# First loads, regrouped heads, a new order, and the rows of maxima issued by ScalarE

## The chip, the core and the metric

One core of one Trainium2 chip. The metric is the device time of one execution in microseconds (us), lower is better. The kernel before takes 883.62 us (median of three runs, 883.47 to 884.68).

## What is computed

Two transformer layers over x of shape (4, 512, 256), batch j being one of four sequences, 16 heads of 16 channels, MLP width 1024. Both layers modulate their norms by a condition vector per batch:

```python
# layer 0
g1, g2, s1, s2, sh1, sh2 = split(silu(cond) @ ada_w.T + ada_b, 6)
h = layernorm(x) * (1 + s1) + sh1
q, k, v = split(h @ qkv_w.T + qkv_b); q, k = rope(q), rope(k)
x = x + (softmax(q k^T / 4) v @ proj_w.T + proj_b) * g1
h2 = layernorm(x) * (1 + s2) + sh2
x = x + (gelu(h2 @ fc1_w.T + fc1_b) @ fc2_w.T + fc2_b) * g2
# layer 1: shift1, scale1, shift2, scale2 = split(swiglu(cond @ w_t1 + b_t1) @ w_t2 + b_t2, 4)
x = x + mha(rmsnorm(x, g1) * (1 + scale1) + shift1)      # rope on even/odd channels
x = x + swiglu(rmsnorm(x, g2) * (1 + scale2) + shift2 ...) @ w_fo + b_fo
```

## The kernel before

**Units and quads.** The work is 8 units (a batch in a layer: units 0 to 3 are layer 0, 4 to 7 layer 1), and each unit's attention is 4 quads of 4 heads, 32 quads in all. A unit has a part before attention (`pre_pieces`: norm, the products qk and v, rope), the quads, and a part after (`post_pieces`: output projection, residual, norm, MLP). The steady schedule runs a unit's quads beside the post part of the unit before and the pre part of the unit after.

**A quad.** TensorE makes 16 products `peaks` (L805), of which VectorE takes a row maximum each into `top` (L1066). `top_turn` (L780) transposes these, ScalarE copies the result into `top_t` (L1280), and two small transfers write it as one more row of the stacked q in `qt`, one for each half of the partitions (`top_row`, L716). 16 products `scores` (L792) then give q k^T with the maximum subtracted, ScalarE takes the exponential (L1290) into `pr`, which has room for 8, and TensorE accumulates `values` (L819) in `ps_o`. `output` copies, transposes (L830) and divides.

**Rope and the round trip.** Heads are grouped for rope in two pairs of chunks. Per pair: ScalarE takes the two chunks (`take`, L1261), VectorE and GpSimd multiply by cosine and sine (L1044, L1381), VectorE adds (L1053), ScalarE makes the high part (`high`, L1271), GpSimd the low part (L1392), and SP spills them to DRAM in four transfers (`spill`, L691 and L694). `fill(n)` reads quad n from there into `qt` and `kt`, which have room for three quads (L708). In the kernel before each quad takes two heads of either pair, so the fill of a unit's first quad waits for both pairs.

**Buffers.** Six PSUM banks (`ring`) are handed to the products in the order of the program; each engine waits for the one it needs by counts.

**Order.** `program()` (L438) is one list of pieces, each with its engine. Every engine runs its own pieces strictly in the order of that list, so a wait on one piece holds all later pieces of the same engine. The list is `first_pieces`, `first_steps`, and then all pieces with hand-given ticks (`QUAD_AT`, `PRE_AT`, `POST_AT`, `SPLIT_AT`), sorted; a quad advances by SQ = 28 ticks.

**The start.** A first block (`prologue`, L1459 to L1515) issues 16 loads on SP, fills constants, and computes silu(cond) and its broadcasts `wide`. It ends for all engines together. Then the main block begins with `mod_0` (L953, 32 matmuls of the modulation), the norm of unit 0, `gates` (L916, one per batch), qk, v, `net_1` and `net_2` (L927, L941: layer 1's condition network).

Of the kernel before, what the change touches and what calls it, by code (L numbers as in the profile page):

```python
# [12 lines left out]
P = 128  # L13
# [85 lines left out]
SQ = 28  # L99
# [8 lines left out]
def first_pieces():  # L108

    def gates(b):  # L110
        return [("pe", "gates", b), ("dve", "gates", b)]

    pieces = [("dve", "norm_stats", 0, 0), ("dve", "norm_var", 0, 0), ("pool", "root", 0, 0),
              ("dve", "norm_rows", 0, 0), ("pe", "mod_0"), ("dve", "mod_0")]
    pieces += gates(0) + [("pe", "norm_turn", 0, 0)] + gates(1)
    pieces += [("act", "modulated", 0, 0, k) for k in range(KC)]
    for pair in range(2):
        for c in (2 * pair, 2 * pair + 1):
            pieces += [("pe", "qk", 0, c), ("act", "take", 0, c)]
        pieces += rope_pieces(0, pair)  # L120
    pieces += [("sp", "fill", 0), ("sp", "fill", 1)]
    for t in range(T):
        pieces += [("pe", "v", 0, t), ("dve", "take_v", 0, t)]
    pieces += gates(2) + [("pe", "net_1")]
    return pieces


def first_steps():

    beside = {0: [("dve", "net_1"), ("act", "net_gate"), ("pe", "gates", 3)],  # L130
              1: [("dve", "net_gate")], 3: [("dve", "gates", 3)],
              3 + NET_PARTS: [("dve", "net_2")]}
    steps = [("sp", "load_x", 2)]
    for i in range(T * QUAD):
        steps.append((None, "peaks", 0, i))
        steps += beside.get(i, [])
        if 2 < i < 3 + NET_PARTS:
            steps.append(("pe", "net_2", i - 3))
    return steps + [("sp", "load_x", 3)] + top_pieces(0)


def top_pieces(n):

    return [("pe", "top", n), ("act", "top", n), ("sp", "top", n)]


def quad_pieces(n):
# [20 lines left out]
PRE_AT = ({'norm': (-80, -50, -19, -33, -12, -8, -2),  # L168
  'qk': (-5, 4, 11, 30),
  'v': (14, 23, 29, 64),  # L170
  'take': (1, 4, 26, 29),
  'take_v': (15, 26, 26, 59),
  'rope': ((8, -4, 11, 12, -2, 9), (38, 40, 39, 45, 50, 37))},
 {'norm': (-10, -1, -17, 4, 9, 12, 12),
  'qk': (14, 14, 25, 28),
  'v': (14, 15, 16, 19),
  'take': (12, 12, 27, 31),
  'take_v': (14, 17, 18, 21),
  'rope': ((18, 9, 19, 25, 13, 22), (28, 18, 34, 44, 48, 66))},
 {'norm': (-12, -3, -1, 7, 10, 10, 10),  # L180
  'qk': (17, 17, 22, 22),
  'v': (22, 23, 24, 24),
  'take': (16, 17, 21, 23),
  'take_v': (22, 23, 24, 24),
  'rope': ((17, 27, 18, 21, 30, 39), (35, 27, 36, 41, 50, 52))})
# [3 lines left out]
POST_AT = ({'o': (-1, -1, -1),  # L189
  'project': (1, 6, 8, 8),  # L190
  'proj': (9, 4, 9, 4),
  'norm': (14, 16, 11, 21, 32, 32, 32),
  'split': (38, 38, 37, 43),
  'up': (41, 41, 45, 45, 50, 50, 56, 60, 67, 68, 75, 76, 85, 86, 92, 93),
  'after_up': (0, 2, 2, 5, 2),
  'down': (47, 50, 53, 56, 61, 64, 71, 74, 82, 82, 84, 92, 97, 98, 106, 111),
  'after_down': (1, 5)},
 {'o': (-1, -1, -1),
  'project': (3, 10, 10, 10),
  'proj': (9, 10, 10, 15),  # L200
  'norm': (16, 16, 26, 19, 29, 25, 27),
  'split': (30, 35, 39, 43),
# [1379 lines left out]
```

## Time and profile before

| | us |
|---|---|
| median of 3 runs | 883.62 |
| profiled execution | 884.96 |
| its span, first to last instruction | 883.2 |

```profile
## 1 busy us (share of the span) xinstructions
PE 804.7 (91%) x4800; PEld 493.7 (56%) x4800; DVE 636.5 (72%) x1348; ACT 491.3 (56%) x1015; POOL 290.4 (33%) x263
## 2 busy tenths in 40 slices
PE   2908999899999999999999999999999999999497
DVE  3225864679897889887988788888868788864344
ACT  0200555556874687558665777766547655666132
PEclk9955786799999999999999999999999999999799
## 4 chain that ended last, share of the span: by engine, by line
PE 71%; DVE 11%; issue 6%; POOL 4%; DMA 3%; ACT 2%; SPq 1%; POOLq 0%; DVEq 0%; ACTq 0%
```

PE is TensorE, PEld its weight loads, DVE VectorE, ACT ScalarE, POOL GpSimd, SPq the SP queue that issues transfers. In part 2 each digit is the busy share of a slice of 22 us in tenths, and PEclk the clock that TensorE was granted in tenths of full speed (10 shows as 9). The first two and a half slices and the slices 3 to 9 are where the rows differ from the rest. Part 4 shares out the chain of work that ended last.

### The profile page before, as it was taken

To read this page: it belongs to the slowest core of one execution; us is meant where nothing else is said; L and a number is where in the kernel's file an instruction comes from. 1 tells how busy PE (TensorE), PEld (TensorE's weight loads), DVE (VectorE), ACT (ScalarE), POOL (GpSimd) and SP (SyncE) were. 2 spreads that over 40 slices of the span, in tenths; PEclk is the share of its full clock that TensorE was granted. 3 is DMA by queue.
4 is the path that set the end of the run, shared out by engine and by line. 5 is a ranking of instruction groups with operands and counts; after the bars stand their busy time and mean duration, and the time that the engine had idled before them with its cause. 6 is when DMAs were issued, how large, how long until landed. Compare 5 with 4: busy or idle time off the path is not lost.

```text
span 883.2 us, 14213 instructions
## 1 busy us (share of the span) xinstructions
PE 804.7 (91%) x4800; PEld 493.7 (56%) x4800; DVE 636.5 (72%) x1348; ACT 491.3 (56%) x1015; POOL 290.4 (33%) x263
## 2 busy tenths in 40 slices
PE   2908999899999999999999999999999999999497
PEld 2504333254665466556654666466856775677396
DVE  3225864679897889887988788888868788864344
ACT  0200555556874687558665777766547655666132
POOL 0310131034345433443345333631244222222234
PEclk9955786799999999999999999999999999999799
DMA  8372244414411441144114413453104502100000
GB/s 318 118 215 55 70 134 130 99 48 132 134 37 37 132 132 37 40 129 132 38 37 131 133 38 85 128 148 73 37 26 132 148 21 60 37 2 1 24 2 25
DMA packets 33480, 76.26 MB, mean 86 GB/s; under 512 B 4480, under 2 KB 9216, under 8 KB 33024
## 3 DMA queue, kind: packets, MB, share of 16 engines
q1 hardware_dynamic: 33408, 75.35, 30.4%
q8 instruction: 39, 0.64, 0.3%
q14 instruction: 33, 0.27, 0.1%
HBM read 39.42 MB, written 35.65 MB: 85 GB/s over the span
## 4 chain that ended last, share of the span: by engine, by line
PE 71%; DVE 11%; issue 6%; POOL 4%; DMA 3%; ACT 2%; SPq 1%; POOLq 0%; DVEq 0%; ACTq 0%
PE ring L888 16%; PE ps_o L819 12%; PE ps_b L905 11%; PE ring L805 8%; PE ring L792 8%; DVE top L1066 6%; PE ring L757 4%; PE ring L858 3%; POOL sines L1381 2%; PE ring L770 2%; PE ring L830 1%; DMA scratch<-low 1%; DMA kt<-scratch 1%; PE ring L739 1%; PE ring L916 1%
## 5 line engine op out<-in xcount | busy, mean ns | idle before, releaser
L1066 DVE TENSOR_REDUCE top<-ring 128x1 f32<-128x512 f32 x512 | 322.4, 682 | 71.1 <-PE ring L805 69.7
L1290 ACT ACTIVATE pr<-ring 128x512 f32<-128x512 f32 x512 | 268.5, 608 | 71.7 <-PE ring L792 62.0
L1422 POOL TENSOR_TENSOR act_l<-mlp,act_h 128x256 fp32r<-128x256 f32 x128 | 100.7, 787 | 270.3 <-DVE act_h L1143 270.3
L805 PE MATMUL ring<-kt,qt 48*128 48x512 f32 x512 | 136.9, 482 | 26.4 <-DMA kt<-scratch 23.4
L819 PE MATMUL ps_o<-pr,va 128*17 128x512 f32 x1024 | 143.1, 645 | 0.2
L792 PE MATMUL ring<-qt,kt 49*128 49x512 f32 x512 | 126.4, 470 | 6.8 <-DMA qt<-top_t 2.5
L805 PEld LDWEIGHTS ring<-kt,qt 48*128 48x128 f32 x512 | 59.4, 195 | 105.5 <-issue 68.0
L1324 ACT ACTIVATE mlp<-ring,col 128x256 f32<-128x256 f32 x128 | 61.2, 478 | 99.7 <-PE ring L888 73.5
L792 PEld LDWEIGHTS ring<-qt,kt 49*128 49x128 f32 x512 | 55.3, 192 | 74.9 <-issue 48.3
L888 PE MATMUL ring<-hh,wl 128*128 128x256 f32 x384 | 83.5, 299 | 5.9 <-issue 3.5
L905 PE MATMUL ps_b<-wh,act_l 128*128 128x256 f32 x256 | 79.8, 312 | 1.2 <-POOL act_l L1422 0.8
L1129 DVE SCALAR_TENSOR_TENSOR mlp<-mlp 128x256 f32<-128x256 f32 x128 | 56.7, 443 | 33.3 <-ACT mlp L1329 30.2
L888 PE MATMUL ring<-hh,wh 128*128 128x256 f32 x384 | 78.3, 286 | 0.0
L888 PE MATMUL ring<-hl,wh 128*128 128x256 f32 x384 | 78.3, 286 | 0.0
L905 PE MATMUL ps_b<-wl,act_h 128*128 128x256 f32 x256 | 72.2, 282 | 0.0
L905 PE MATMUL ps_b<-wh,act_h 128*128 128x256 f32 x256 | 72.0, 281 | 0.0
L888 PEld LDWEIGHTS ring<-hh,wl 128*128 128x128 f32 x384 | 60.0, 193 | 21.0 <-issue 16.4
L1381 POOL TENSOR_TENSOR sines<-raw,trig 128x1024 f32<-128x1024 f32 x16 | 44.9, 2807 | 61.1 <-ACT raw L1261 30.1
L905 PEld LDWEIGHTS ps_b<-wh,act_l 128*128 128x128 f32 x256 | 48.5, 189 | 26.9 <-issue 24.1
L888 PEld LDWEIGHTS ring<-hh,wh 128*128 128x128 f32 x384 | 60.9, 195 | 0.0
L888 PEld LDWEIGHTS ring<-hl,wh 128*128 128x128 f32 x384 | 60.6, 194 | 0.0
L757 PE MATMUL ring<-hf,wf 128*128 128x512 f32 x128 | 59.5, 604 | 0.0
(91 smaller groups left out, 1038.2 us busy)
## 6 DMA issues: line engine op xcount, KB each, us to landing
scratch<-high SPq DMA_DIRECT2D x48, 512.0 KB, 5.0
qt<-scratch SPq DMA_DIRECT2D x64, 192.0 KB, 3.5
kt<-scratch SPq DMA_DIRECT2D x64, 192.0 KB, 4.4
scratch<-low SPq DMA_DIRECT2D x16, 512.0 KB, 5.9
mlp<-in_w_split SPq DMA_DIRECT2D x20, 256.0 KB, 3.2
xs<-in_x SPq DMA_DIRECT2D x4, 512.0 KB, 8.4
wf<-in_w_f SPq DMA_DIRECT2D x2, 1024.0 KB, 11.7
out_x<-xs SPq DMA_DIRECT2D x4, 512.0 KB, 2.9
```

The lines of the kernel that those rows point to most:

```text
L757: last = nc.tensor.matmul(bank[:, :], w[:, k, c * P:(c + 1) * P], hf[:, k, :], start=(k == 0), stop=(k == KC - 1))
L792: nc.tensor.matmul(bank[:, :], kt[r:r + SHIFT + 1, n % NSLOT, h // 2, t * P:(t + 1) * P], qt[r:r + SHIFT + 1, n % NSLOT, h // 2, :], start ...
L805: nc.tensor.matmul(bank[:, :], qt[r:r + SHIFT, n % NSLOT, h // 2, t * P:(t + 1) * P], kt[r:r + SHIFT, n % NSLOT, h // 2, :], start=True, s ...
L819: last = nc.tensor.matmul(ps_o[32 * h:32 * h + HD + 1, :], va[:, u % 2, t, QUAD * g + h, :], pr[:, slot, :], start=(t == 0), stop=(t == T ...
L888: last = nc.tensor.matmul(bank[:, s * TH:(s + 1) * TH], wp[:, k, c:c + P], hp[:, k, half * TH:(half + 1) * TH], start=(n == 0), stop=(n == ...
L905: last = nc.tensor.matmul(ps_b[:, s * C:(s + 1) * C], ap[:, at % 2, s * P:(s + 1) * P], wp[:, f, :], start=(f == 0 and s == 0 and n == 0), ...
L1066: nc.vector.tensor_reduce(top[:, n % 2, c:c + 1], bank[:, :], AX_X, ALU.max, negate=True).then_inc(free, 1)
L1129: step(nc.vector.scalar_tensor_tensor(val[at % 2], aux[at % 2], 1.0, val[at % 2], ALU.add, ALU.mult))
L1290: nc.scalar.activation(pr[:, at % NP, :], bank[:, :], ACT.Exp, scale=SCALE).then_inc(free, 1)
L1324: nc.scalar.activation(val[at % 2], src, ACT.Identity, bias=col[:, c:c + 1]).then_inc(val_in, 1)
L1381: nc.gpsimd.tensor_tensor(sines[:, :, :], raw[:, :, :], trig[:, 1, :].unsqueeze(1).to_broadcast([P, 2, L]), ALU.mult).then_inc(sin_in, 1)
L1422: nc.gpsimd.tensor_tensor(act_l[:, at % 2, :], src, act_h[:, at % 2, :].bitcast(F32), ALU.subtract).then_inc(act_l_in, 1)
```

## The change

**First loads.** The prologue's block issues 6 loads only, in a new order: cond, x of batch 0, the first third of the modulation weights (now stored so that norm 1's scale and shift come first), cols, identity, and the qkv weights of layer 0. The other loads are pieces of SP's program (`load`). `mod_0` is split in two halves of 16 matmuls. silu, `half_gate` and the broadcasts `wide` (`widen`) become pieces. The weights of the condition network and of the gates move to other buffers, with a semaphore each.

**Regrouping.** The heads of the qkv weights are reordered so that pair 0 holds the heads of quads 0 and 1 and pair 1 those of quads 2 and 3. Fill n waits for the spill of its own pair only.

**Order.** All tick tables are new, with 112 ticks to a quad. The first pieces and all loads have ticks of their own (`FIRST_AT`, `LOAD_AT`) and are sorted in with the rest. TensorE's list now begins mod_0(0), norm_turn(0), qk 0, qk 1, v 0, v 1, qk 2, net_1, v 2, mod_0(1), qk 3, net_2(0), net_2(1), v 3, gates 0 to 3, net_2(2), net_2(3), peaks of quad 0 (with the rest of net_2 between them). SP's begins trig, ada1, ada2, wf0, t1, w_split 0, row, grow, t2, spill(0,0), x1, fill(0), w_split 1, fill(1), spill(0,1). TensorE's last stretch, from the last exponentials on, keeps its sequence but for a few `up` and `down` steps that trade places.

**Rows of maxima.** The piece ("sp", "top") is gone. ScalarE, after its copy into `top_t`, waits for that copy and issues both transfers itself.

The diff, cut to its core (the tick tables left out):

```diff
-SQ = 28
+SQ = 112
...
-    return [("pe", "top", n), ("act", "top", n), ("sp", "top", n)]
+    return [("pe", "top", n), ("act", "top", n)]
...
-    out = []
+    out = [(tick, *piece) for tick, piece in zip(FIRST_AT, first_pieces())]
+    out += [(tick, "sp", "load", name) for name, tick in LOAD_AT.items()]
...
-    return first_pieces() + first_steps() + [p[1:] for p in sorted(ticked(), key=lambda p: p[0])]
+    return [p[1:] for p in sorted(ticked(), key=lambda p: p[0])]
...
+                def load(name):
+
+                    if name in ("x1", "x2", "x3"):
+                        j = int(name[1])
+                        if j == 2:
+                            sp.wait_ge(*filled("net_1"))
+                        if j == 3:
+                            sp.wait_ge(*filled("gates", B - 1))
+                        sp.dma_start(xs[:, j], x_v[j]).then_inc(x_in[j], 16)
+                    elif name == "wf1":
+
+                        sp.wait_ge(*filled("net_2"))
+                        sp.dma_start(wf[:, NWF // 2:NWF], w_f32[:, NWF // 2:NWF]).then_inc(s_wf[2], 16)
...
                     u, g = quad_of(n)
-                    if g == 0:
-                        for pair in range(2):
-                            sp.wait_ge(*spill_landed(u, pair))
+                    sp.wait_ge(*spill_landed(u, g // 2))
...
-                                         scratch[u % 2, :, 8 * op + 2 * g + e, op:op + 3].rearrange(
+                                         scratch[u % 2, g // 2, 2 * op + g % 2, :, e, op:op + 3].rearrange(
                                              "a s d f t -> (s d f) a t")).then_inc(slot_in[n % NSLOT], 16)
-
-                def top_row(n):
-
-                    sp.wait_ge(*emptied("top", n))
-                    for e in range(2):
-                        sp.dma_start(qt[STACK * e + SHIFT:STACK * e + SHIFT + 1, n % NSLOT, :, :].bitcast(F32),
-                                     top_t[8 * e:8 * e + 8, n % 2, :].bitcast(F32)).then_inc(top_in[n % 2], 16)
...
-                def mod_0():
+                def mod_0(m):
...
-                    pe.wait_ge(s_ada, 16)
-                    for n in range(4 * KC):
+                    pe.wait_ge(s_ada[m], 16)
+                    for n in range(2 * KC):
...
                     nc.scalar.activation(top_t[:, n % 2, :], bank[0:T * QUAD, 0:P], ACT.Copy).then_inc(free, 1)
+                    ac.wait_ge(free, before + 1)
+                    for e in range(2):
+                        nc.scalar.dma_start(qt[STACK * e + SHIFT:STACK * e + SHIFT + 1, n % NSLOT, :, :].bitcast(F32),
+                                            top_t[8 * e:8 * e + 8, n % 2, :].bitcast(F32)).then_inc(top_in[n % 2], 16)
...
+            sp.dma_start(cond, cond_t.rearrange("p (k b) -> p k b", k=KC)).then_inc(s_small[0], 16)
             sp.dma_start(xs[:, 0], x_v[0]).then_inc(x_in[0], 16)
+            sp.dma_start(ada[:, :, 0:2 * C], ada_v[:, :, 0:2 * C]).then_inc(s_ada[0], 16)
+            sp.dma_start(col[:, :], cols).then_inc(s_small[1], 16)
+            sp.dma_start(eye[:, :], ident).then_inc(s_small[2], 16)
+            sp.dma_start(wf[:, 0:PROJ[0]], w_f32[:, 0:PROJ[0]]).then_inc(s_wf[0], 16)
...
-                for g in range(NQ):
-                    for e in range(2):
-                        h = g * QUAD + pair * 2 + e
-                        order.append(op * C + h * HD + halves[layer][half * HALF:(half + 1) * HALF])
+                for h in range(2 * QUAD * pair, 2 * QUAD * (pair + 1)):
+                    order.append(op * C + h * HD + halves[layer][half * HALF:(half + 1) * HALF])
```

## Rows read from the trace of the kernel before

**Rows 1.** Busy time by stage: window, its length, each engine, PEclk, DMA, GB/s

```profile
0.00:16.16 16.16, 0.00 (x1) 0.03 (x1) 4.96 (x15) 1.49 (x2) 0.55 (x7) 1.00 0.81 290
16.16:44.20 28.04, 27.62 (x100) 18.85 (x100) 9.38 (x23) 5.03 (x7) 8.87 (x5) 1.00 0.48 177
44.20:64.75 20.55, 0.01 (x2) 0.03 (x1) 4.74 (x8) 1.06 (x1) 2.78 (x2) 0.51 0.73 215
64.75:90.03 25.28, 19.60 (x57) 11.76 (x58) 14.19 (x32) 0.48 (x2) 0.00 (x0) 0.57 0.25 62
90.03:183.31 93.28, 84.99 (x334) 33.88 (x335) 62.10 (x115) 50.17 (x96) 12.24 (x6) 0.75 0.40 107
183.31:272.00 88.69, 87.59 (x544) 51.68 (x544) 76.05 (x165) 62.53 (x134) 37.64 (x34) 1.00 0.33 88
820.00:883.20 63.20, 45.09 (x320) 42.63 (x320) 27.48 (x69) 16.09 (x36) 22.05 (x24) 0.87 0.05 18
```

**Rows 2.** The same view over two longer stretches

```profile
64.75:183.31 118.56, 104.59 (x391) 45.64 (x392) 76.30 (x146) 50.65 (x98) 12.24 (x6) 0.71 0.37 98
183.31:820.00 636.69, 627.40 (x3990) 386.54 (x3989) 513.62 (x1092) 416.98 (x872) 243.86 (x220) 0.99 0.29 78
```

**Rows 3.** Timeline of the first block: start, length, engine, line, operation

```profile
0.72 0.40 SPq L1465 DMA_DIRECT2D o<-in_cond_t  x1
1.19 0.41 SPq L1465 DMA_DIRECT2D col<-in_cols  x1
...
4.64 0.27 DVE L1504 MEMSET top<- 128x256 f32 x1
...
15.28 0.43 SPq L1476 DMA_DIRECT2D wf<-in_w_f  x1
```

**Rows 4.** Waits of TensorE for transfers: total us, times, longest; whole span, then 183 to 820

```profile
PE ring L805 <- DMA kt<-scratch: 23.4, 2, 20.5
...
PE ring L792 <- DMA qt<-top_t: 0.6, 1, 0.6
```

**Rows 5.** The chain of waits from 16 to 66 us: start, length, what

```profile
16.16 6.96 PE ring L953 x32
...
29.80 3.45 PE ring L757 x8
...
42.78 5.89 DMA scratch<-low
...
52.58 5.99 DMA scratch<-low
...
59.98 4.63 DMA kt<-scratch
```

**Rows 6.** Busy time, as rows 1, of two short stretches of the first loads

```profile
4.00:8.00 4.00, 0.00 (x0) 0.00 (x0) 1.01 (x4) 0.10 (x1) 0.00 (x0) 1.00 1.00 290
8.00:12.00 4.00, 0.00 (x0) 0.00 (x0) 1.49 (x11) 0.11 (x1) 0.00 (x0) 1.00 0.99 397
```

**Rows 7.** Timeline of the setup of unit 0, 17 to 72 us

```profile
17.59 0.38 DVE L994 BATCH_NORM_AGGREGATE mv<-stats 128x2 f32<-128x6 f32 x4
19.45 1.38 DVE L1015 TENSOR_SCALAR xn<-xs,mv,rstd 128x256 f32<-128x256 f32 x4 [1.48 <-POOL rstd L1370]
22.98 3.76 PE L916 MATMUL ring<-pr,o 128*128 128x512 f32 x4
23.16 0.19 DVE L1205 TENSOR_TENSOR o<-ring,col 128x32 f32<-128x32 f32 x1 [2.32 <-PE ring L953]
26.53 1.54 PE L739 MATMUL ring<-eye,xn 128*128 128x128 f32 x8
27.70 1.45 ACT L1247 ACTIVATE hf<-ring,mod 128x512 f32<-128x512 f32 x2 [19.59 <-PE ring L739]
27.91 1.88 PE L916 MATMUL ring<-pr,o 128*128 128x512 f32 x4
31.55 0.69 ACT L1261 ACTIVATE raw<-ring,col 128x512 f32<-128x512 f32 x1 [2.41 <-PE ring L757]
36.50 3.62 PE L770 MATMUL ring<-wf,hf 128*128 128x256 f32 x16
42.36 1.84 PE L927 MATMUL ring<-o,xs 128*128 128x4 f32 x16
71.48 0.68 DVE L1164 TENSOR_TENSOR gate<-ring,add 128x512 f32<-128x512 f32 x1
```

**Rows 8.** The issues of the rows of maxima: ns min/median/max, first and last start

```profile
L716 SPq DMA_DIRECT2D qt<-top_t x64: 623/646/774, 87.3 to 801.4; - x64
L1280 ACT ACTIVATE top_t<-ring x32: 249/251/268, 87.0 to 800.5; 16x128 fp32r<-16x128 f32 x32
```

**Rows 9.** SP's longest wait (total, times, longest), and one landing in the chain

```profile
SPq L716 <- ACT top_t L1280: 390.2, 31, 31.1
...
287.80 2.52 DMA qt<-top_t
```

More of the change, by code:

```diff
@@ L108, in first_pieces @@
 def first_pieces():
[L110 to L115, printed above, removed]
+    pieces = [("act", "silu"), ("dve", "half_gate"), ("dve", "silu"), ("pe", "mod_0", 0), ("dve", "norm_stats", 0, 0),
+              ("dve", "norm_var", 0, 0), ("pool", "root", 0, 0), ("dve", "mod_0", 0), ("dve", "norm_rows", 0, 0),
+              ("pe", "norm_turn", 0, 0)]
     pieces += [("act", "modulated", 0, 0, k) for k in range(KC)]
@@ L119, in first_pieces @@
             pieces += [("pe", "qk", 0, c), ("act", "take", 0, c)]
[L120 to L139, printed above, removed]
+        pieces += rope_pieces(0, pair) + [("sp", "fill", pair)]
+        if pair == 0:
+            for t in range(T):
+                pieces += [("pe", "v", 0, t), ("dve", "take_v", 0, t)]
+    pieces += [("pe", "mod_0", 1), ("dve", "mod_0", 1)]
+    for b in range(B):
+        pieces += [("dve", "widen", b), ("pe", "gates", b), ("dve", "gates", b)]
+    pieces += [("pe", "net_1"), ("dve", "net_1"), ("act", "net_gate"), ("dve", "net_gate")]
+    return pieces + [("pe", "net_2", part) for part in range(NET_PARTS)] + [("dve", "net_2")]
+FIRST_AT = (-1462,
+ -798,
+ -1447,
+ -1309,
+ -1227,
+ -1155,
+ -1302,
+ -1156,
+ -1101,
+ -1172,
+ -1416,
+ -1230,
+ -1145,
+ -829,
+ -1042,
+ -808,
+ -1053,
+ -1090,
+ -865,
+ -801,
+ -780,
+ -746,
+ -656,
+ -910,
+ -835,
+ -892,
+ -816,
+ -815,
+ -666,
+ -608,
+ -601,
+ -887,
+ -669,
+ -725,
+ -488,
+ -644,
+ -611,
+ -595,
+ -487,
+ -604,
+ -601,
+ -608,
+ -763,
+ -668,
+ -833,
+ -543,
+ -600,
+ -670,
+ -525,
+ -527,
+ -600,
+ -523,
+ -464,
+ -589,
+ -471,
+ -413,
+ -816,
+ -696,
+ -702,
+ -652,
+ -668,
+ -626,
+ -417,
+ -411,
+ -337,
+ -322,
+ -261,
+ -165,
+ -156)
 def top_pieces(n):
-    return [("pe", "top", n), ("act", "top", n), ("sp", "top", n)]
+    return [("pe", "top", n), ("act", "top", n)]
 def quad_pieces(n):
@@ L414, in pieces_beside @@
     if u == 0:
[L415 removed]
+        out += split_pieces(range(NPLACE), SPLIT_AT[0])
     if u == B + 1:
[L418 to L419 removed]
+        out += split_pieces(range(NPLACE, NCHUNK), SPLIT_AT[1])
     if u >= 1:
@@ L1452, in name @@
     def name(n):
         return sem("pre_" + n)
-    s_small, s_ada, s_t, s_row = (name(n) for n in ("small", "ada", "t", "row"))
-    s_wf = [name("wf0"), name("wf1")]
-    fill, silu_in, dve = (name(n) for n in ("fill", "silu_in", "dve"))
+    s_small = [name("cond"), name("col"), name("eye")]
+    s_ada = [name(f"ada{i}") for i in range(3)]
+    s_wf = [name(f"wf{i}") for i in range(3)]
+    fill = name("fill")
     with nc.Block() as block:
```

597 lines of the change are left out of this document (316 added, 281 removed).

## The prediction

> **What bounds the kernel now.** I read the span by stages first [rows 1]. The table cuts it where the work changes, and the reader is to see four regimes. From 0 to 16.16 us TensorE does nothing. From 16.16 to 44.20 it is busy with the first unit's setup. From 44.20 to 64.75 it is idle again, and its granted clock stands at the lower of its two levels. From 64.75 to 183.31 (attention of unit 0) it is nominally busy 104.6 of 118.6 us, but at a mean clock of 0.71 [rows 2]. From 183.31 to 820 it is busy 627.4 of 636.7 us at 0.99: there TensorE is the bound and only 9.3 us are idle. The last 63.2 us are a chain for the last unit. So whatever does not cut TensorE's own work can win only in the first 183 us, and can lose anywhere.
>
> Next I read what ends the idle stretches. At 16.16 TensorE and VectorE both start, although nothing they need arrives then: the SP queue has just issued its sixteenth load (15.28 plus 0.43 us), and the first program block ends for all engines together [rows 3]. At 64.75 the releaser is a transfer into kt; 20.5 us of TensorE's 23.4 us of waiting on such transfers lie here [rows 4]. The chain behind it [rows 5] runs: hf of unit 0 written by 29.15, pair 0 rotated and spilled (landed 48.67), then pair 1 (landed 58.57), and only then the fills, because the old fill of a unit's first quad waits for both pairs.
>
> **Part 1, the first loads.** After the change the first block issues 6 loads, not 16. At the 0.47 us spacing of these issues [rows 3] they end near 3.5 us; VectorE's three memsets end at 4.91 [rows 3], so the block ends near 5.2. x of batch 0 and the first third of the modulation weights are the second and third load, 1.0 MB together. At the 397 GB/s of the 8 to 12 us stretch [rows 6] that is 2.6 us, and with the slower start of the 4 to 8 us stretch I put the second of them at 7.0. The product mod_0 then has 16 matmuls, not 32: half of 6.96 us [rows 5], done at 10.5. VectorE's three small operations on it take about 0.5 us (estimate: the first of them starts 0.2 after the product and takes 0.19 [rows 7]). Its order puts the variance behind them, so 11.0. From there norm_var to the end of norm_rows took 3.24 us (17.59 to 20.83), and turn to the end of hf 2.62 us (26.53 to 29.15) [rows 7]: 16.9, against 29.15. Gain 12.2 us; the gate product that stood ahead of the turn is moved behind. One thing is paid back. The same four gate matmuls took 3.76 us at 22.98 and 1.88 at 27.91 [rows 7], so TensorE ran at half speed for its first 10 us or so, whatever the clock column says there. Now it starts with less work and gaps, and qk 0 and 1 (3.45 us at full speed, twice that at half) will be met in part: I add 2.0 us, between nothing and 3.45. The nine loads issued by SP from its program, 4.6 MB or 12 us at that rate, end near 20 us, before the first spill; the price if they did not is in the rivals.
>
> **Part 2, regrouping.** Quads 0 and 1 now need only rope pair 0. The first fill no longer waits from 48.67 to 58.57 [rows 5]: 9.9 us. The sizes of spills and fills stay. Sum of parts 1 and 2: first peaks at 64.75 - 12.2 + 2.0 - 9.9 = 44.7. What is late next is TensorE itself. After qk 0 and 1 (near 22.4) it has v (3.62 us), qk 2 and 3 (3.45 [rows 5]), net_1 (1.84 for 16 small matmuls), the second mod_0 (16 of the same kind, 1.84), four gates (4 x 1.88) and half of net_2 (16 more, 1.84): 20.1 us [rows 7], so until 42.5. It fits, and the idle 20.55 us of before are filled. For units 1 to 7 the same relaxation is worth nothing: in 183 to 820 the rows show no wait of TensorE for a fill.
>
> **Part 3, the attention of unit 0.** The stage of 118.56 us holds 76.3 us of VectorE work [rows 2]; a gate (0.68 us [rows 7]) and net_1's small ones leave it, some 1.3 us: 75.0. In the steady stage VectorE is busy 76.05 of 88.69 us, 86% [rows 1]: by that share the stage takes 87.5 us. TensorE's work there is 19.6 x 0.57 + 85.0 x 0.75 = 75 us of full clock, less 3.7 for a gate and half of net_2 that left: 71. At the old mean of the main part, 0.75, it takes 95 us. The lower clock followed the long idle stretch, which is gone, but with VectorE pacing the peaks TensorE will still stand idle in pieces, and the rows show the clock at 0.75 for 93 us after the idle stretch had long ended. So I take 92, between the two and nearer the second. Gain 26.6 us. Ends: 84 us if VectorE reaches 90%, and 114 us if it stays at the 67% (62.10 of 93.28) of before.
>
> The Trainium skill, "TensorE: Matmul & The Clock Gate", section "HAM oscillation — how this bites in real kernels", says that a kernel whose matmuls come in bursts between waits keeps falling back to the lower clock; the low rows of 64.75 to 183.31 agree. By that rule alone the stage would stay as long as before; that is the first rival below.
>
> **Part 4, the rows of maxima on ScalarE.** 64 transfers leave SP. Each issue took 646 ns (623 to 774) on SP [rows 8]. SP waited 390 us for these copies [rows 9], with fills, spills and weight loads queued behind; those now pass. But TensorE waited for a row only 0.6 us in 183 to 820 [rows 4], so nothing is returned. The new cost lies on ScalarE: per quad two issues (1.29 us) and a wait for its own copy (0.26 us): 1.55 us, 50 us over 32 quads. No row shows an issue on ScalarE, so this is bounded by SP's. Behind the wait are the next exps, and TensorE waits for their banks. ScalarE is busy 62.53 of 88.69 us and would come to 68.7, still 20 us short of TensorE, and by the new ticks the copy stands some 55 of a quad's 112 ticks, 11 us, ahead of the scores that need its row. Ends for the 28 steady quads: nothing, or the whole 1.55 each, 43 us. It is nearest to the first, since TensorE's idle time there is 9.3 us in all though ScalarE works through its list in 0.6 us steps and more all the while [rows 7]: I take 0.2 per quad, 6 us.
>
> The landing itself took 2.52 us after the issue [rows 9]. The Trainium skill, "DMA: Bandwidth & Descriptors", section "Issuing engines are not separate DMA queues", speaks against this part: another issuing engine saves only issue time. By it this part is worth 0 or less, as taken.
>
> **Part 5, the new order.** All ticks are new and four times as fine; all 1.5% of idle time in the steady stage is what it can return, and a bad order can cost as much. Between -9 and +9 I take -3. The tail's order on TensorE hardly differs (a few up and down steps trade places), so its 63.2 us stay: 0.
>
> **The sum**: 883.2 - 12.2 + 2.0 - 9.9 - 26.6 + 6 - 3 = 839.5 us of span. The profiled execution took 884.96, the median of the runs is 883.62, 0.4 above the span. Forecast: 840 us.
>
> **The rivals.**
> First, the clock stays low: VectorE keeps 67%, the stage takes 114 us: gain 4.6 instead of 26.6, so 862. For it: the clock rows. Against: part of the low clock followed one idle stretch that goes.
> Second, ScalarE's blocks reach TensorE in part: 0.8 us per steady quad, 22 us instead of 6: 856. For it: ScalarE sits between TensorE's scores and TensorE's values in both directions.
> Third, slower than before: each of the 32 rows stalls TensorE for its whole block and one more hand-over, together over 1.6 us. Without part 4 the sum is 833.5; 32 x 1.6 = 51 gives 885, so from 1.6 us per row it decides, and at 1.75 it is 890. Against: 20 us of free ScalarE time in each unit.
> Fourth, better: the stage takes 84 us, ScalarE costs nothing, and the order returns 6: 883.2 - 20.1 - 34.6 - 6 = 822.5, so 823.
> Fifth, the change doesn't do what it says at the start: the loads put on SP stand in front of the first spill, or TensorE's filling work runs over, and the 9.9 us are lost: 850.
>
> **How the numbers follow.** Forecast (832 to 849) 0.50; first rival 0.15; second 0.12; third 0.04; fourth 0.13; fifth 0.06. The range leaves out the third and the outer part of the fourth and first: 822 to 861. A difference of 0.2%, 1.8 us, is about what a measurement can tell here; all cases but the third are faster: 0.95 faster, 0.01 same, 0.04 slower.
>
> **What would show it.** VectorE's first norm_stats near 6 us, hf of unit 0 near 17, the first peaks near 45, with TensorE busy until then: parts 1 and 2. The first projection of unit 0 (183.31 before) near 137: part 3; if near 159, the clock, to be seen as a mean near 0.75 and VectorE at 67%. From there to the end of the attention near 637 us again; if it is 650 or more and TensorE waits on exps just behind the copies of the row of maxima, part 4 was sized wrong. Issues on ScalarE's queue far from 0.65 us would move that term. It would all be wrong if the new order makes an engine wait in line for something late, which no row of before can show.

## The result, and the profile after

The changed kernel takes 843.38 us (median of 4 runs, 839.93 to 845.36), against 884.15 for the kernel before in the same job (883.47 to 885.35): ratio 0.9533, 95% interval 0.9497 to 0.957. The forecast was 840 with a range of 822 to 861. The profiled execution took 844.6 us with a span of 842.7. In the experiments below the medians and ranges as measured are of all runs and the ratios of the fast ones; four_issues and one_issue have one slow run each (884.43 and 829.1), without which their medians are 873.5 and 821.58, and every price worked out for them goes by these two.

I cut the span at the same points of the work as before: first `peaks`, first `project`, last turn of an output. The lines of the stages of after (core 0; stretch, its length, busy time and instructions of TensorE, its weight loads, VectorE, ScalarE and GpSimd, then granted clock, share of the DMA queues, GB/s):

```profile
0.00:7.03 7.03, 0.00 (x0) 0.00 (x0) 3.77 (x6) 1.49 (x2) 0.55 (x7) 1.00 0.67 207
7.03:46.15 39.12, 32.24 (x121) 21.09 (x121) 15.68 (x53) 7.03 (x10) 14.08 (x8) 0.96 0.70 233
46.15:135.21 89.06, 81.15 (x370) 35.92 (x370) 71.17 (x131) 49.77 (x95) 8.33 (x6) 0.81 0.54 158
135.21:780.24 645.03, 621.73 (x3991) 387.86 (x3991) 517.93 (x1091) 417.31 (x873) 245.23 (x220) 0.98 0.28 78
780.24:842.66 62.42, 43.98 (x322) 41.84 (x320) 28.00 (x70) 16.07 (x36) 22.27 (x24) 0.88 0.05 18
```

and the steady stretch of the kernel before, cut at the same turn (which is 0.7 us before the end of the longer one in [rows 2]):

```profile
183.31:819.30 635.99, 627.12 (x3989) 386.50 (x3989) 513.27 (x1090) 416.98 (x872) 243.86 (x220) 0.99 0.29 78
```

| stage | before | forecast | after |
|---|---|---|---|
| to the first peaks | 64.75 | 44.7 | 46.15 |
| attention of unit 0 | 118.6 | 92 | 89.1 |
| steady stretch | 636.0 | 639 | 645.0 |
| last part | 63.9 | 63.9 | 62.4 |

So 48 us came out of the first two stages and 9 went back in the steady one. There TensorE stands idle for 23.3 us, where it was 8.9 before. What it waits for in that stretch (engine and line that wait, what they wait for: us in total, times, longest):

```profile
PE ring L886 <- DMA qt<-top_t: 4.0, 2, 3.3
PE ps_o L913 <- ACT pr L1425: 3.2, 5, 1.0
PE ring L899 <- ACT mlp L1466: 2.5, 3, 0.8
PE ps_b L999 <- POOL act_l L1569: 2.2, 4, 1.0
PE ring L982 <- POOL hl L1562: 2.0, 4, 0.8
PE ring L886 <- DVE mlp L1242: 1.5, 2, 0.8
```

L886 is now `scores`, L899 `peaks`, L913 `values`, L982 and L999 the two MLP products. ScalarE (ACT) is behind the second and third row, and it feeds the engines in the fourth and sixth. It now also issues the rows of maxima of the first row. One quad in the timeline of ScalarE (start, duration, engine, line, operation, and in brackets idle time before it):

```profile
290.17 0.42 ACT L1475 ACTIVATE mlp<-mlp 128x256 f32<-128x256 f32 x1 [0.67 <-DVE mlp L1255]
290.58 0.27 ACT L1411 ACTIVATE top_t<-ring 16x128 fp32r<-16x128 f32 x1
290.88 1.32 ACTq L1414 DMA_DIRECT2D qt<-top_t  x2
292.32 0.47 ACT L1462 ACTIVATE mlp<-ring,col 128x256 f32<-128x256 f32 x1 [1.47 <-DVE act_h L1248]
```

From the end of the copy to ScalarE's next instruction pass 1.47 us, nearly all of them issuing. This is no harmless place: the chain of work that ended last runs through both issues here and on into the MLP's activation (start, us, what):

```profile
290.58 0.27 ACT top_t L1411
...
290.88 0.66 ACTq L1414
...
291.57 0.63 ACTq L1414
...
292.69 0.47 ACT mlp L1466
```

Part 4 of the page gives ACTq, ScalarE's queue, 3% of the span (the line of these issues, L1414, has 2% there), where the kernel before had 0%:

```profile
PE 65%; DVE 11%; ACT 6%; issue 5%; DMA 4%; POOL 4%; ACTq 3%; SPq 1%; POOLq 0%; DVEq 0%
```

2 to 3% of 843 is 17 to 25 us, where my sum had 6. The total was right, so something else must have been worth more than I gave it. That is what the experiments had to take apart.

### The profile page after: what moved, and what is told of

It reads as the page before. It is cut to its first block, busy times and chain, and to the rows that moved or that the text cites. A ratio compares the mean times of both kernels' runs of the same rounds, so it can differ in the third digit from the quotient of the medians.

```text
span 842.7 us, 14249 instructions
## 1 busy us (share of the span) xinstructions
PE 779.1 (92%) x4800; PEld 486.7 (58%) x4800; DVE 636.5 (76%) x1349; ACT 491.7 (58%) x1015; POOL 290.4 (34%) x263
## 4 chain that ended last, share of the span: by engine, by line
PE 65%; DVE 11%; ACT 6%; issue 5%; DMA 4%; POOL 4%; ACTq 3%; SPq 1%; POOLq 0%; DVEq 0%
PE ring L982 15%; PE ps_o L913 11%; PE ps_b L999 8%; PE ring L899 8%; PE ring L886 7%; PE ring L851 6%; DVE top L1171 6%; PE ring L952 3%; PE ring L864 3%; ACTq L1414 2%; ACT pr L1425 2%; DMA qt<-top_t 2%; POOL sines L1528 1%; DMA kt<-scratch 1%; POOL hl L1562 1%
## 5 line engine op out<-in xcount | busy, mean ns | idle before, releaser
L913 PE MATMUL ps_o<-pr,va 128*17 128x512 f32 x1024 | 136.8, 617 | 3.2 <-ACT pr L1425 3.2
L899 PE MATMUL ring<-kt,qt 48*128 48x512 f32 x512 | 129.3, 471 | 7.4 <-ACT mlp L1466 2.5
L886 PE MATMUL ring<-qt,kt 49*128 49x512 f32 x512 | 121.6, 465 | 9.8 <-DMA qt<-top_t 7.3
L899 PEld LDWEIGHTS ring<-kt,qt 48*128 48x128 f32 x512 | 58.8, 195 | 75.6 <-issue 41.4
L886 PEld LDWEIGHTS ring<-qt,kt 49*128 49x128 f32 x512 | 53.5, 190 | 83.7 <-issue 55.0
L982 PE MATMUL ring<-hh,wl 128*128 128x256 f32 x384 | 84.5, 303 | 7.9 <-issue 3.5
L999 PE MATMUL ps_b<-wh,act_l 128*128 128x256 f32 x256 | 78.2, 306 | 3.1 <-POOL act_l L1569 3.0
L982 PE MATMUL ring<-hl,wh 128*128 128x256 f32 x384 | 79.7, 290 | 0.0
L982 PE MATMUL ring<-hh,wh 128*128 128x256 f32 x384 | 79.7, 290 | 0.0
L982 PEld LDWEIGHTS ring<-hh,wl 128*128 128x128 f32 x384 | 61.5, 198 | 24.6 <-issue 12.5
L999 PE MATMUL ps_b<-wl,act_h 128*128 128x256 f32 x256 | 72.4, 283 | 0.0
L999 PE MATMUL ps_b<-wh,act_h 128*128 128x256 f32 x256 | 72.3, 282 | 0.0
L851 PE MATMUL ring<-hf,wf 128*128 128x512 f32 x128 | 66.2, 658 | 1.3 <-ACT hf L1376 1.3
L982 PEld LDWEIGHTS ring<-hh,wh 128*128 128x128 f32 x384 | 62.3, 199 | 0.0
L982 PEld LDWEIGHTS ring<-hl,wh 128*128 128x128 f32 x384 | 62.2, 199 | 0.0
L999 PEld LDWEIGHTS ps_b<-wh,act_l 128*128 128x128 f32 x256 | 49.0, 191 | 19.8 <-issue 17.5
```

Of the source, the lines that this page charges most:

```text
L851: last = nc.tensor.matmul(bank[:, :], w[:, k, c * P:(c + 1) * P], hf[:, k, :], start=(k == 0), stop=(k == KC - 1))
L886: nc.tensor.matmul(bank[:, :], kt[r:r + SHIFT + 1, n % NSLOT, h // 2, t * P:(t + 1) * P], qt[r:r + SHIFT + 1, n % NSLOT, h // 2, :], start ...
L899: nc.tensor.matmul(bank[:, :], qt[r:r + SHIFT, n % NSLOT, h // 2, t * P:(t + 1) * P], kt[r:r + SHIFT, n % NSLOT, h // 2, :], start=True, s ...
L913: last = nc.tensor.matmul(ps_o[32 * h:32 * h + HD + 1, :], va[:, u % 2, t, QUAD * g + h, :], pr[:, slot, :], start=(t == 0), stop=(t == T ...
L982: last = nc.tensor.matmul(bank[:, s * TH:(s + 1) * TH], wp[:, k, c:c + P], hp[:, k, half * TH:(half + 1) * TH], start=(n == 0), stop=(n == ...
L999: last = nc.tensor.matmul(ps_b[:, s * C:(s + 1) * C], ap[:, at % 2, s * P:(s + 1) * P], wp[:, f, :], start=(f == 0 and s == 0 and n == 0), ...
```

## The experiments

Each kernel was timed in five rounds beside the kernel before, whose median in the three jobs was 883.63, 883.91 and 885.12 us. All but one start from the changed kernel. The milestones of all profiled executions stand in one table behind the single results; each row of it, and every trace shown, is of one execution.

### SP issues again: rows_on_sp

```diff
-    return [("pe", "top", n), ("act", "top", n)]
+    return [("pe", "top", n), ("act", "top", n), ("sp", "top", n)]
...
+                def top_row(n):
+                    sp.wait_ge(*emptied("top", n))
+                    for e in range(2):
+                        sp.dma_start(qt[...], top_t[...]).then_inc(top_in[n % 2], 16)
...
-                    ac.wait_ge(free, before + 1)
-                    for e in range(2):
-                        nc.scalar.dma_start(qt[...], top_t[...]).then_inc(top_in[n % 2], 16)
```

> The changed kernel with the rows of maxima issued by SP again (the piece for SP comes back at the third tick of the tables); everything else stays. Theory A (my part 4: an issue on ScalarE costs TensorE little, and gives nothing back): 6 us less than the changed kernel, 837, with the stretch from the first projection to the last turn of o near 640 instead of 646. Theory B (the new order itself is the loser of the 9 us in that stretch, ScalarE's issues cost nothing): 843. Theory C (the rows on their own queue are what lets SP's fills pass and is worth something): over 848.

Measured: 815.51 us (815.24 to 818.06), ratio 0.9225 (0.9202 to 0.9249), which none of the three theories had. ScalarE's issuing costs 27.9 us, 0.87 per quad, more than four times my term. And without it the steady stretch is 14.9 us shorter than before, not 3:

```profile
50.40:130.60 80.20, 76.08 (x370) 34.13 (x370) 70.72 (x132) 49.08 (x95) 9.23 (x7) 0.87 0.50 150
130.60:751.70 621.10, 612.37 (x3990) 384.66 (x3991) 513.96 (x1091) 417.19 (x873) 245.78 (x220) 0.99 0.30 83
```

TensorE is idle for 8.7 us of the second stretch, no less than in the kernel before (8.9). The whole gain of the new order lies in time that counted as busy: 627.1 then, 612.4 now, for the same matmuls within one. The granted clock is not the reason, 0.99 in both. Added up one by one, the groups of matmuls of the stretch take some 954 us then and 947 now (they overlap): about half of the 14.7 us is shorter matmuls, those of `scores` and `peaks` above all (203.8 to 198.4 us together), the rest more overlap between them. Why they got shorter, no run shows. The two groups in the kernel before, then in rows_on_sp (busy us, mean ns, idle before):

```profile
L805 PE MATMUL ring<-kt,qt 48*128 48x512 f32 x423 | 102.5, 458 | 1.0 <-DVE top L1066 0.6
L792 PE MATMUL ring<-qt,kt 49*128 49x512 f32 x444 | 101.3, 455 | 3.3 <-ACT hf L1247 1.2 <-DMA qt<-top_t 0.6 <-DVE top L1066 0.4
```

```profile
L893 PE MATMUL ring<-qt,kt 49*128 49x512 f32 x444 | 99.6, 452 | 2.1 <-DMA qt<-top_t 1.8
L906 PE MATMUL ring<-kt,qt 48*128 48x512 f32 x424 | 98.8, 451 | 2.4 <-DMA kt<-scratch 1.1 <-DVE o L1195 0.9 <-ACT hf L1383 0.2
```

A busy TensorE is not TensorE at its peak. The weight loads hardly moved (386.5 and 384.7 us, 61% and 62% of the stretch), so they never said that it was full. The Trainium skill, "Perfetto Trace Analysis", section "Identifying the Most-Contended Engine", calls matmul busy time a poor measure of how near the engine is to its limit, and names the share of weight loads as one of two to use instead. These rows agree: I had taken 98.5% busy as a ceiling on what an order could return.

### ScalarE's issues alone: rows_on_act_alone

The kernel before with only the issues moved to ScalarE, and its own loads, grouping and order.

```diff
-    return [("pe", "top", n), ("act", "top", n), ("sp", "top", n)]
+    return [("pe", "top", n), ("act", "top", n)]
...
+                    ac.wait_ge(free, before + 1)
+                    for e in range(2):
+                        nc.scalar.dma_start(qt[...], top_t[...]).then_inc(top_in[n % 2], 16)
```

> The kernel before with only the rows of maxima moved to ScalarE: old loads, grouping and order. Theory A: 32 quads at 0.2 us each, 884 to 892, most likely 890. Theory C (own queue helps): below 882. If each block of 1.55 us reached TensorE it would be 930.

Measured: 902.11 us (898.68 to 905.19), ratio 1.0202 (1.0173 to 1.023). Alone, this part of the change is a loss of 18.5 us, more than twice the 8 that theory A allowed at most. It costs less than the 27.9 in the new order, and the trace offers a reason: in the kernel before ScalarE had nothing to do for 0.54 us (median of 32) behind the copy, in rows_on_sp its next instruction follows without a gap.

### More issues, and fewer: four_issues and one_issue

four_issues adds two transfers of `top_t` to HBM behind the two to `qt`. one_issue writes both rows with one transfer, since the two partitions are 64 apart:

```diff
...
-                    for e in range(2):
-                        nc.scalar.dma_start(qt[STACK * e + SHIFT:STACK * e + SHIFT + 1, n % NSLOT, :, :].bitcast(F32),
-                                            top_t[8 * e:8 * e + 8, n % 2, :].bitcast(F32)).then_inc(top_in[n % 2], 16)
+                    nc.scalar.dma_start(qt[SHIFT:SHIFT + STACK + 1:STACK, n % NSLOT, :, :].bitcast(F32),
+                                        top_t[:, n % 2, :].bitcast(F32)).then_inc(top_in[n % 2], 16)
```

> The changed kernel with two more transfers of the same rows per quad, issued by ScalarE behind the first two and written to an unused place in DRAM: the issue time on ScalarE doubles, 1.3 us more for each of 32 quads. Theory A: at 0.2 us per 1.55 us of block, or somewhat more since the slack is used up, 849 to 860. Theory B: within 3 us of the changed kernel, 843. If ScalarE's time went over to TensorE in full: 885.

> The changed kernel with both rows of a quad in a single transfer on ScalarE, which writes partitions 48 and 112 at once: one issue instead of two, 0.63 us less of ScalarE per quad, 20 us of its time in all. Theory A: 2 to 4 us less than the changed kernel, 840. Theory B: no change, 843.

Measured: 875.23 us (867.57 to 884.43), ratio 0.9875 (0.983 to 0.9919), and 823.05 us (815.86 to 829.1), ratio 0.9274 (0.9238 to 0.9311). Both lie outside what any theory named. One issue fewer gives back 21.8 of the 27.9 us, two more cost another 30.1. So the price does not go by the number: 6 us for the first issue, 22 for the second, 15 for each of the two more (which are shorter, 476 ns in the median). The one transfer of one_issue took no longer to issue than one of the two (minimum, median, maximum in ns; after, then one_issue):

```profile
L1414 ACTq DMA_DIRECT2D qt<-top_t x64: 627/627/1472, 59.9 to 761.1; - x64
```

```profile
L1413 ACTq DMA_DIRECT2D qt<-top_t x32: 507/518/1122, 60.9 to 742.2; - x32
```

### Is it the wait, the second transfer, or ScalarE's time: own_wait_c, one_on_sp_c, other_work_c

own_wait_c is rows_on_sp with ScalarE's wait for its own copy and nothing behind it. one_on_sp_c is rows_on_sp with the single transfer of one_issue. other_work_c has five small copies to an unused place behind the wait:

```diff
...
+                    ac.wait_ge(free, before + 1)
+                    ac.wait_ge(s_trig, 16)
+                    flat = trig[:, :, :].rearrange("p w t -> p (w t)")
+                    for i in range(5):
+                        nc.scalar.activation(spare[:, 80 * i:80 * i + 80], flat[:, 0:80], ACT.Copy)
```

> rows_on_sp (815.5 us) with only ScalarE's wait for its own copy at that place, and no work behind it. Theory D (the time of the issues costs): 816 to 822. Theory F (the wait, which empties ScalarE's pipeline, is what costs): over 830.

> rows_on_sp (815.5 us) with both rows of maxima of a pair in one transfer, still issued by SP. If only the time that ScalarE spends on issuing is paid for, nothing changes: within 2 us of 815.5. If the landing of the second transfer also matters, it is a little faster, about 813.

> rows_on_sp (815.5 us) with ScalarE waiting for its own copy of the maxima and then writing five 80-column copies to an unused place, about 1.3 us of ordinary work where the changed kernel has its two issues; SP still issues the transfers. Theory D (any time of ScalarE at that place costs): 840, like the changed kernel. Theory E (it is something about issues on ScalarE's queue): 817 to 822.

Measured: own_wait_c 815.44 us (810.38 to 817.14), ratio 0.9215 (0.9181 to 0.925): the wait costs nothing, theory F falls. one_on_sp_c 812.03 us (809.93 to 814.78), ratio 0.9188 (0.9156 to 0.922): the best of all kernels here and near the 813 of the second theory, though its interval overlaps that of rows_on_sp. other_work_c 824.51 us (822.36 to 830.8), ratio 0.9336 (0.9298 to 0.9374): 9 us, between what theories D and E named. The trace says why: ScalarE overlaps its copies, so five of 0.25 us are over after 0.91, and the next instruction starts 0.82 after the first of them. This was not the 1.3 us that I had meant to test.

### The same time as ordinary work: nine_copies_b

other_work_c with nine copies in place of five.

> other_work_c with nine 80-column copies (to two-byte numbers) in place of five. In other_work_c the five took 0.91 us from first start to last end and 0.82 us to the next instruction, since ScalarE overlaps them, against 1.31 and 1.44 for the changed kernel's two issues; nine should take about 1.5. Costs per quad so far, over own_wait_c or rows_on_sp: 0.68 us of ScalarE 0.25, 0.91 us 0.3, 1.31 us 0.87, 2.6 us 1.87. Theory D, now with a slack (ScalarE has about 0.5 us to spare at that place, and what is over is paid in full): 838 to 846. Theory E (copies are cheap, issues are dear): 828 to 832, twice the cost of five copies without a bend.

Measured: 837.08 us (834.76 to 838.0), ratio 0.9451 (0.942 to 0.9482). Nine copies in the timeline, between the copy of the maxima and the next activation:

```profile
286.37 0.27 ACT L1419 ACTIVATE top_t<-ring 16x128 fp32r<-16x128 f32 x1
286.67 1.55 ACT L1424 ACTIVATE spare<-trig 128x80 bf16<-128x80 f32 x9
288.12 0.45 ACT L1471 ACTIVATE mlp<-ring,col 128x256 f32<-128x256 f32 x1
```

Five copies cost 9 us, nine cost 21.6: 1.8 times the number, 2.4 times the price. The bend that D asks for is there; its figure (838 at least) is just missed. Plain work of the length of the two issues costs 21.6 us where they cost 27.9, so about three quarters of the price is that of ScalarE's time, whatever fills it.

### Issues without a reader: idle_issues_b

own_wait_c with two issues per quad whose transfers go to HBM and are never read; SP issues the rows.

```diff
...
+                    for e in range(2):
+                        nc.scalar.dma_start(spare[n, e], top_t[8 * e:8 * e + 8, n % 2, :].bitcast(F32)
+                                            ).then_inc(spare_in[n % 2], 16)
```

> own_wait_c (815.4 us) with two issues per quad on ScalarE whose transfers go to a place in HBM that nobody reads; SP still issues the rows of maxima. Theory D (the time of ScalarE is what is paid for): 838 to 846, like the changed kernel. Theory G (the rows of maxima land later when ScalarE issues them, and TensorE waits for that): 817 to 830.

Measured: 827.89 us (822.41 to 828.9), ratio 0.9336 (0.9302 to 0.937). By the number theory G would win. The trace takes most of that back. These issues were much shorter than those of the rows:

```profile
L1426 ACTq DMA_DIRECT2D spare<-top_t x64: 269/274/537, 64.0 to 745.1; - x64
```

so ScalarE lost 0.85 us per quad (next instruction 0.76 behind the end of the copy, against 0.09 ahead of it in rows_on_sp), as with the five copies, and paid the like. Nor does ScalarE issue the rows later: from the end of the copy to the end of the second issue pass mostly 1.31 to 1.35 us on ScalarE and 1.33 to 1.44 on SP.

A part of G holds all the same: the rows can land later. TensorE's waits for them (four, one and one; us in total, times, longest) in the changed kernel, in nine_copies_b, which has a hole of the same length, and here:

```profile
PE ring L886 <- DMA qt<-top_t: 7.3, 4, 3.3
```

```profile
PE ring L894 <- DMA qt<-top_t: 1.0, 1, 1.0
```

```profile
PE ring L897 <- DMA qt<-top_t: 0.7, 1, 0.7
```

The longest of them, in the changed kernel (the chain that ended last, then SP's own list at that time), and the same place in nine_copies_b:

```profile
472.08 0.63 ACTq L1414
...
472.74 5.39 DMA qt<-top_t
...
478.27 0.50 PE ring L886 x2
```

```profile
470.75 3.16 SPq L792 DMA_DIRECT2D scratch<-high  x3
```

```profile
467.62 0.63 SPq L816
...
468.29 3.02 DMA qt<-top_t
...
471.44 0.50 PE ring L894 x2
```

```profile
467.62 1.30 SPq L816 DMA_DIRECT2D qt<-top_t  x2
468.96 3.10 SPq L793 DMA_DIRECT2D scratch<-high  x3
```

When SP issues the rows, its list puts them ahead of the spills, which are 512 KB each; when ScalarE does, the first of the spills go out ahead of them, and the rows take 2.4 us longer to land. The other long wait of the changed kernel (2.7 us, at 80.74) is alike: SP issues fills at 74.57, the rows follow at 75.04, and landing takes 4.88 us; in nine_copies_b the fills stand behind the rows (81.91, 80.47). The waits for rows differ by 6.3 us between the two kernels, and so do their times. No run holds SP's transfers back behind ScalarE's rows, so that this is the cause is argued and not shown.

### All kernels on one line

"Hole" is the median time from the end of the copy of the maxima to ScalarE's next useful instruction, over 32 quads.

| kernel | behind the copy on ScalarE | hole, us | time, us | above 815.5, per quad |
|---|---|---|---|---|
| one_on_sp_c | nothing | -0.09 | 812.03 | -0.11 |
| rows_on_sp | nothing | -0.09 | 815.51 | 0 |
| own_wait_c | wait | 0.03 | 815.44 | 0 |
| one_issue | one issue | 0.66 | 821.58 | 0.19 |
| idle_issues_b | two short issues | 0.76 | 827.89 | 0.39 |
| other_work_c | five copies | 0.85 | 824.51 | 0.28 |
| changed kernel | two issues | 1.45 | 843.38 | 0.87 |
| nine_copies_b | nine copies | 1.48 | 837.08 | 0.67 |
| four_issues | four issues | 2.31 | 873.5 | 1.81 |

Whatever stands in the hole, its length orders the times, within some 3 us at equal length (6 between the changed kernel and nine_copies_b). The price is bent: nothing for the wait, 0.3 to 0.5 of a hole of 0.66 to 0.85, 0.45 to 0.60 of one of 1.45 to 1.48, and from there to 2.31 about as much as the hole itself grows (0.94 for 0.86). The 6 us at 1.45 are as much as the changed kernel's longer waits for the rows, above. four_issues and one_issue also scatter most (within 16.9 and 13.2 us); the changed kernel (5.4) does so no more than own_wait_c (6.8).

### The start: both_pairs_c and long_block_b

both_pairs_c is rows_on_sp with the first two fills behind the second spill, as the kernel before has them (in SP's list too, by a few lines of `program()` left out here):

```diff
...
-                    sp.wait_ge(*spill_landed(u, g // 2))
+                    sp.wait_ge(*spill_landed(u, 1 if u == 0 else g // 2))
```

long_block_b is rows_on_sp with nine of the loads back in the first program block.

> rows_on_sp (815.5 us) with unit 0's first two fills put behind the second spill, as the kernel before has its fill behind both pairs: the regrouping of the first block half undone. By part 1 of my sum the first peaks come near 57 to 60 us instead of 50.4 and the whole is 821 to 826. Rival: unit 0's stage absorbs it and the time stays within 3 us of 815.5.

> rows_on_sp (815.5 us) with nine of the loads that the change puts behind the first block moved back into it (3.8 MB and more, at about 300 to 400 GB/s some 10 us of the queues). By part 1 of my sum the first peaks come 5 to 12 us later than 50.4 and the whole is 820 to 828. Rival: the loads of x and of the first weights go first on all queues anyway, so the start does not move and the time stays within 3 us of 815.5.

Measured: both_pairs_c 823.14 us (821.0 to 826.45), ratio 0.9321 (0.9285 to 0.9357), first peaks at 60.6, just above the 57 to 60 of the expectation. TensorE waits where it did before:

```profile
PE ring L910 <- DMA kt<-scratch: 13.1, 1, 13.1
```

The first peaks come 10.2 us later and the whole is 7.6 longer, so the regrouping is worth most of its 9.9 us from [rows 5]. The 10.2 is of two executions, and this start varies by up to 5 us from one to the next (below); the 7.6 is of medians. long_block_b takes 816.9 us (815.84 to 818.87), ratio 0.9233 (0.9202 to 0.9263): my expectation fell, and the rival there holds, but not for its reason. The start did move. First statistics and hand-over to TensorE in rows_on_sp:

```profile
6.90 1.40 DVE L1095 BATCH_NORM_STATS2 stats<-xs 128x6 f32<-128x256 f32 x4
7.03 3.57 PE L1063 MATMUL ring<-small,pr 128*128 128x4 f32 x16 [7.03 <-DVE small L1338]
```

and in long_block_b:

```profile
10.87 1.40 DVE L1111 BATCH_NORM_STATS2 stats<-xs 128x6 f32<-128x256 f32 x4
11.01 3.58 PE L1079 MATMUL ring<-small,pr 128*128 128x4 f32 x16 [11.01 <-DVE small L1354]
```

Four us later at the start, 1.4 later at the first peaks, 1.4 at the end, which is within the scatter. In rows_on_sp it is TensorE that is late at the first peaks, busy with setup until then, and how long that setup takes depends on the clock (below).

### Who paces unit 0: twice_peaks_b

rows_on_sp with each of unit 0's 64 `peaks` matmuls issued twice.

```diff
...
+                    if n < NQ:
+                        nc.tensor.matmul(bank[:, :], qt[r:r + SHIFT, n % NSLOT, h // 2, t * P:(t + 1) * P],
+                                         kt[r:r + SHIFT, n % NSLOT, h // 2, :], start=True, stop=True)
                     nc.tensor.matmul(bank[:, :], qt[r:r + SHIFT, n % NSLOT, h // 2, t * P:(t + 1) * P],
                                      kt[r:r + SHIFT, n % NSLOT, h // 2, :], start=True, stop=True).then_inc(full, 1)
```

> rows_on_sp (815.5 us) with the peaks' matmuls of unit 0 (its four quads) issued twice: 64 more matmuls of 0.38 to 0.49 us, 24 to 31 us of TensorE's work, all in unit 0's attention stage, which takes 80.2 us with TensorE busy 76.1 of them, much of it at the lower clock. If VectorE paces that stage (70.7 us busy) and TensorE's idle and slow time is slack, the time moves by less than 4 us. If TensorE paces it, the stage grows by 15 us or more. Rival: the added work keeps the clock up and the stage grows by 7 us or less.

Measured: 816.22 us (813.97 to 820.91), ratio 0.9229 (0.9197 to 0.9261). The 64 added matmuls lengthen the stage by 4.7 us in the one execution profiled, the slowest of the six, and the whole by 0.7 in the median; the clock in the stage is 0.88 against 0.87, so they did not pay for themselves by keeping it up. My 24 us for them was too much, since matmuls in a row overlap: four `peaks` at 47.11 in the changed kernel took 0.78 us together, by which 64 take some 12 (estimate). Even so most of it vanished: TensorE's busy time in the stage grew by 5.7 us, and at most 4.7 of the 12 were paid. So TensorE does not pace unit 0 by itself. With VectorE busy 70.7 of 80.2 us (88%) the stage is mostly VectorE's, and what TensorE loses there by its low clock is in large part hidden; how large, one profiled execution does not settle.

The milestones, in us, with the stages between them:

| kernel | first peaks | unit 0 | steady | last | span |
|---|---|---|---|---|---|
| before | 64.7 | 118.6 | 636.0 | 63.9 | 883.2 |
| rows_on_act_alone | 64.8 | 118.2 | 657.4 | 62.5 | 902.9 |
| changed kernel | 46.1 | 89.1 | 645.0 | 62.5 | 842.7 |
| rows_on_sp | 50.4 | 80.2 | 621.1 | 62.1 | 813.8 |
| one_on_sp_c | 50.3 | 80.6 | 618.5 | 63.0 | 812.4 |
| own_wait_c | 45.7 | 80.8 | 619.9 | 62.2 | 808.6 |
| one_issue | 47.4 | 82.2 | 631.2 | 63.8 | 824.6 |
| idle_issues_b | 50.2 | 81.3 | 632.3 | 62.6 | 826.4 |
| other_work_c | 47.4 | 78.6 | 632.1 | 62.6 | 820.7 |
| nine_copies_b | 49.8 | 82.7 | 639.3 | 63.4 | 835.2 |
| four_issues | 47.6 | 88.0 | 667.9 | 62.3 | 865.8 |
| both_pairs_c | 60.6 | 78.3 | 620.2 | 62.2 | 821.3 |
| long_block_b | 51.8 | 77.8 | 621.7 | 63.1 | 814.4 |
| twice_peaks_b | 50.6 | 84.9 | 620.2 | 63.4 | 819.1 |

## Why the prediction was right, and where only its sum was

The forecast of 840 stood 3.4 us from the median, but two of its five terms were far off with opposite signs. That the total came so near is luck as far as these two go.

**Part 1, the first loads: right in its steps, and later found to be worth less than its gain.** Statistics at 6.89 (forecast 7.0 for their data), product mod_0 at 7.03 and 3.58 long (3.48), hf whole at 17.20 (16.9), qk 0 and 1 in 5.83 us (5.45 with the added 2.0). What I had not seen is the cover behind it: with the regrouping in place, four of those microseconds were worth 1.4 (long_block_b). The other 8 were not tried alone.

**Part 2, the regrouping: right.** First peaks at 46.15 against 44.7, with TensorE busy until 44.9 and 1.2 us of waiting for the fill behind that; both_pairs_c gives 10.2 us at the first peaks and 7.6 in the whole. The fifth rival did not come: the loads put on SP held up no spill that anyone waited for.

**Part 3, unit 0: right in size, and for half the reason.** 89.1 us against 92. My two models gave 87.5 (VectorE at the steady stretch's share) and 95 (TensorE at the old clock), and I leant to the second. twice_peaks_b speaks for the first. (By the 75.0 us of VectorE's work and the shares that I named, the ends are 83 and 113, not 84 and 114.) Without ScalarE's issues the stage takes 80.2, beyond the better end; with them it stands at 89.1. These 8.9 us belonged to part 4 only in part: nine_copies_b has the same hole and takes 82.7 (2.5 more than rows_on_sp), 3.3 us are TensorE's waits for rows in the stage, against 0.3 in rows_on_sp, and the rest goes with a lower mean clock, 0.81 against 0.87, whose cause is open. The mean clock rose from 0.71 to 0.81 and 0.87, against the rival that had it stay low.

**Part 4, issuing on ScalarE: the mechanism was named, its size was wrong by 22 us.** The issues took 627 ns, as sized from SP's 646 [rows 8], and the block of 1.55 us per quad was right too (1.45 and the 0.09 that it replaces). The step that failed is "It is nearest to the first [end], since TensorE's idle time there is 9.3 us in all though ScalarE works through its list in 0.6 us steps and more all the while", together with "still 20 us short of TensorE". Mean free time of an engine says nothing about an instruction in its list that all later ones must wait for. ScalarE takes exps for `values`, moves results out of PSUM banks that TensorE wants back, and feeds the MLP's second product by way of VectorE and GpSimd, all in strict order, and each hand-over has its own lead. The table of holes shows how little lead there was: a hole of 0.66 to 0.85 us already costs 0.2 to 0.4 per quad, one of 1.5 costs 0.7 to 0.9. By the milestones the changed kernel and rows_on_sp are 8.9 us apart in unit 0, which is part 4's only in part, and 23.9 in the steady stretch; the first peaks, 4.3 us earlier in the former, hide some of this in these two executions (the clock of the start, below). The measured price, 0.87, lies on the second rival (0.8 per quad, 856), which I gave 0.12. Its price was right, its total was not, because of the next point. In the other direction I was right that SP's long waits [rows 9] returned nothing: with SP issuing again nothing is lost. But that "those now pass" was no gift. SP's spills and fills now go ahead of the rows, and the 0.6 us that TensorE waited for rows in the steady stretch [rows 4] became 4.0; in the whole span it was 2.5 and became 7.3.

**Part 5, the order: -3 was -15.** The failed step is "all 1.5% of idle time in the steady stage is what it can return". Idle time was hardly reduced (8.9 to 8.7 us); what shrank is TensorE's busy time, 627.1 to 612.4 for the same matmuls. How this splits over the many moved pieces was not tried.

The two together: I had +6 and -3 outside unit 0, and the steady stretch shows +23.9 and -14.9. Their sums, +3 and +9, look alike. Had I put part 4 right and left part 5 alone, the forecast would have been 862, farther off than the wrong one. One of the two rows in "what would show it" did catch this: the steady stretch came at 645 where 637 was named as right and 650 as the sign of a wrong part 4, and it lay between, because both were wrong.

**The last part** stayed, 63.9 to 62.4.

## What to carry to other kernels

An issue of these rows held the engine that made it for some 0.6 us, so ask what stands behind it in that engine's list. On SP, which computes nothing, it cost this kernel nothing that I could measure; on ScalarE, between hand-overs that TensorE lives on, two in a row cost over half of their length and more the longer the block grew, though the engine was idle for a third of the time. Moving an issue to another engine also changes what is issued ahead of it: here large spills went ahead of small rows that TensorE waited for. Keep such transfers on SP unless something there is really late, and merge them first: one transfer with a stride over partitions did the work of two. And when the bounding engine looks 98% busy, do not take the other 2% as all that an order can give: look at its weight loads, or at how busy time for the same matmuls compares.

## What the hardware showed that I had not expected

**The length of an issue depends on the transfer.** On ScalarE, 8 partitions of `top_t` to one partition of `qt`: 627 ns. All 16 to two partitions 64 apart: 518. 8 partitions to HBM: 274, and 476 behind two of the first kind (four_issues). On SP the first took 650.

**The clock falls at different moments in the same start.** TensorE's work before the first peaks is the same in the changed kernel and in rows_on_sp, and both are idle for 0.9 us between 28 and 32 us. In the first the granted clock then shows its lower level for less than 4 us (mean 0.58 in 32 to 36 us) and is full again; in rows_on_sp it is 0.71, 0.50, 0.50 and 0.58 in the four stretches from 28 to 44. TensorE is busy for 32.2 us in the one and 37.7 in the other for the same work, and the first peaks move from 46.15 to 50.4. Over the ten executions here with this start they fall between 45.7 and 50.6. The total follows only in part. The Trainium skill, "TensorE: Matmul & The Clock Gate", section "What's actually happening", says of the start of a kernel that the number of matmuls at the lower clock varies from run to run. These rows show such a variation further in.

**The clock's record is not to be trusted at the very start.** In the changed kernel it shows 1.00 from 16 to 24 us, while the weight loads of qk 0 and 1 start 0.86 us apart until 21 us and 0.43 apart from there on.
